# Attention turns written out without a loop, one order of stages, and two GpSimd additions in pieces

## The chip, the cores and the metric

The kernel runs on one core of a Trainium2 chip. The metric is the device time of one launch in microseconds (us). Engines are named as the profile names them: PE is TensorE (PEld its weight loads), DVE is VectorE, ACT is ScalarE, POOL is GpSimd, SP is SyncE, which here only issues DMAs.

## The reference, cut to what matters

One language model block over 32 sequences of 512 tokens, 256 features wide, 16 heads of 16 features:

```
h = emb[x] + (lora_A[:, x].T @ lora_B.T) * 2
n = layernorm(h)
q, k, v = split(n @ Wqkv + bqkv)
local  = softmax(q k / 4, only |i - j| <= 64) @ v
glob   = softmax(q k[first 64] / 4) @ v[first 64]
gate   = sigmoid(n @ Wg + bg)
h = h + ((1 - gate) * local + gate * glob) @ Wout + bout
n = layernorm(h)                       # then the routed part
probs = softmax(n @ router_w.T); top 2 of 8 experts, each with a capacity
h = h + n + sum over the 2 of prob * (silu(n @ w1[e]) @ w2[e])
```

## The kernel before, in words

There are three blocks. A short one prepares weights and tables. The second, which the change is about, does embedding, attention and routing, one sequence after another. The third does the eight experts; it keeps its own loops and is not touched.

**Turns.** The second block is a software pipeline. Turn `i` works on six sequences at once: `cur` (i) has its scores, exponentials and outputs, `nxt` (i+1) its queries, keys and row maxima, `far` (i+2) its embedding, `prev` (i-1) its output projection and second norm, `past` (i-2) its routing, `old` (i-3) the writing of its routing table. `turns` runs turns -2 to 3 and 30 to 34 as code written out, and turns 4 to 29 as one loop (`eng.Fori(4, SEQ - 2)`), so its back jump is taken 25 times on each of the five engines. Inside the loop the waits compare a semaphore with a register, and a `sem_inc` on a `carry` semaphore follows many waits on DVE, POOL and SP. These `sem_inc`s also stand in the turns that are written out.

**Order.** Each turn has 20 jobs. `order` yields for job `n` the stages of `BEFORE[n]`, then `exp n`, then a `max`, then a select, a gather or a scatter, then the stages of `AFTER[n]`. Every engine walks the same list and takes from it the stages in which it has a part. Each engine is a queue that executes in order, and semaphores link them.

- `max m`: PE makes band scores into `psS` banks 2 and 3 (L703 to L725), DVE reduces them to row maxima `negm` (L1007, every fifth L1011). PE may not start the next `max` before DVE has read this one.
- `cut g`: four short dependent DVE instructions (L1022, L1025, L1028, L1031) split the maxima of one quarter of the heads into three bf16 parts. `m_rows g`: PE transposes these (L819), ACT copies, SP sends them out and back into the rows that the scores of `exp` read.
- `exp n`: PE scores with the maximum taken off (L745, every fifth L752), ACT exponentiates (L914, L918), POOL zeroes the corners of the band (`sel`, L550 and L552). `out`: PE multiplies with the values (L773, L778).
- `mix q`: PE transposes outputs, DVE scales them (L1106, L1108, L1111), POOL adds the two halves (L585, 128x256).
- `scale 2`, `scale 1`: DVE normalizes `h1` into `x2` (L1202) and `h` into `xn` (L1210), four instructions each. `values`: PE L805. `qk3`: POOL L592.
- `hold`: POOL adds the output bias to `h` for all four token blocks in one instruction (L597, 128x1024). `residual`: POOL adds `x2` to `h1` in one instruction (L602, 128x1024).

In the tables `cut 1`, `cut 2`, `cut 3` and `cut 0` stand in `BEFORE` of jobs 1, 6, 11 and 16, so on DVE each cut comes ahead of the `max` of that job. The `m_rows` of the same number stands in `AFTER` of that job, so on PE it comes behind the same `max`. Between `max 6` and `max 7` of `nxt`, DVE has `scale 1`, and then the last routing instructions (L1093 to L1095).

Of the kernel before, what the change touches and what calls it, by code (L numbers as in the profile page):

```python
# [89 lines left out]
def build(nc, x, emb, lora_a, lora_b, wqkv, bqkv, wout, bout, wg, bg, rw, w1, w2, y):  # L90
# [20 lines left out]
    with outer:  # L111
# [226 lines left out]
        with ExitStack() as mem:  # L338
# [20 lines left out]
            gates = tmp("gates", [P, 2, QB])  # L359
# [73 lines left out]
            k_top, k_rank, k_mix, egate1_done = sem("k_top"), sem("k_rank"), sem("k_mix"), sem("egate1_done")  # L433
            LOADS = 2 * 16
# [6 lines left out]
            def turns(eng, turn):  # L441


                def whole(i):
                    return dict(old=0 <= i - 3 < SEQ, past=0 <= i - 2 < SEQ, prev=0 <= i - 1 < SEQ, cur=0 <= i < SEQ,
                                nxt=0 <= i + 1 < SEQ, far=0 <= i + 2 < SEQ)
# [9 lines left out]
            BEFORE = {  # L456
                1: (("cur", "cut", 1),),
                2: (("prev", "evac", 3),),
                6: (("cur", "cut", 2),),
                9: (("cur", "evac", 0),),  # L460
                11: (("cur", "cut", 3),),
                12: (("cur", "evac", 1),),
                16: (("nxt", "cut", 0), ("norm", "std", None)),
                17: (("cur", "evac", 2),),
            }
            AFTER = {
                0: (("prev", "out", 10), ("cur", "values", 1)),
                1: (("cur", "m_rows", 1), ("prev", "out", 11), ("cur", "values", 2), ("past", "router", None)),
                2: (("nxt", "xn_t", 0), ("nxt", "xn_t", 1), ("past", "top", 0)),
                3: (("cur", "out", 0), ("nxt", "qk", 0), ("nxt", "qk", 1), ("nxt", "qk2", 0), ("nxt", "qk2", 1), ("cur", "kg", 2), ("past", "top", 1)),  # L470
                4: (("nxt", "qk", 2), ("nxt", "qk", 3), ("nxt", "qk2", 2), ("nxt", "qk2", 3), ("nxt", "qk3", 0), ("nxt", "qk3", 1), ("past", "top", 2), ("past", "weights", None)),
                5: (("cur", "out", 1), ("prev", "mix", 0), ("nxt", "qk3", 2), ("nxt", "qk3", 3), ("past", "top", 3)),
                6: (("cur", "m_rows", 2), ("cur", "out", 2), ("prev", "mix", 1), ("past", "top", 4)),
                7: (("prev", "mix", 2),),
                8: (("prev", "mix", 3), ("cur", "kg", 3)),
                9: (("cur", "out", 3), ("cur", "gates", None), ("nxt", "gate", 0), ("past", "top", 5)),
                10: (("cur", "out", 4), ("past", "ahead", None), ("past", "rank", 0), ("prev", "attn_t", 0), ("nxt", "gate", 1)),
                11: (("cur", "m_rows", 3), ("cur", "out", 5), ("prev", "attn_t", 1), ("past", "rank", 1)),
                12: (("prev", "project", 0), ("prev", "project", 1), ("past", "rank", 2)),
                13: (("cur", "out", 6), ("far", "embed", None), ("prev", "stats2", 0), ("nxt", "kg", 0), ("past", "rank", 3)),  # L480
                14: (("far", "lora", 0), ("far", "lora", 1), ("prev", "stats2", 1)),
                15: (("cur", "out", 7), ("far", "stats1", 0), ("far", "stats1", 1)),
                16: (("nxt", "m_rows", 0), ("cur", "out", 8), ("far", "hold", None), ("prev", "scale", 2)),
                17: (("far", "scale", 1), ("past", "rank", 4)),
                18: (("cur", "out", 9), ("prev", "x2_t", 0), ("prev", "x2_t", 1), ("prev", "residual", None), ("nxt", "kg", 1),
                     ("past", "rank", 5)),
                19: (("nxt", "values", 0), ("far", "zgate", None)),
            }
# [6 lines left out]
            def order(on):

                has = lambda flag: on["prev"] or on["far"] if flag == "norm" else on[flag]
                for n in range(JOBS):
                    for flag, stage, arg in BEFORE.get(n, ()):
                        if has(flag):  # L500
                            yield stage, arg
# [1176 lines left out]
```

## Time and profile before

| what | value |
|---|---|
| median of 3 runs | 4374.85 us (4371.02 to 4392.25) |
| the profiled execution | 4373.87 us, of which the span is 4372.2 us |
| PE busy in the span | 3655.6 us (84%) |
| DVE, POOL, ACT busy | 2346.0, 2267.7, 1905.2 us |
| second block | from about 64 us to about 2700 us |

The chain that ended last in the profile starts at about 2700 us, in the third block, so it says nothing of the second. The second block has to be read turn by turn: from one `m_rows` on PE to the same one a turn later, and from what PE waits for in between. `PEclk` is the granted TensorE clock: 1.00 is 2.4 GHz, 0.50 is 1.2 GHz, and a value between is a mean over time at these two.

### The profile page before, as it was taken

The page shows a single profiled execution, that of the slowest core. Times are in us where ns is not written, and L with a number is a line of the kernel's source. Part 1 is how long each engine was busy: PE and PEld are TensorE (multiplying, and loading weights), DVE is VectorE, ACT ScalarE, POOL GpSimd, SP SyncE. Part 2 cuts the span into 40 slices and gives each one's busy share as a digit, 9 for nine tenths or more (in the row PEclk, how much of TensorE's full clock was granted, in tenths as well). Part 3 has the DMA queues.
Part 4 walks back from the last instruction along what each step waited for, and adds up shares of the span by engine and source line. Part 5 has one row for each costly group of instructions (what it writes and reads, how often), then busy time and mean ns, then how long its engine had stood idle before and what let it go on. Part 6 is the DMA issues. An engine that isn't in the chain of part 4 may idle for free. (4 is left out here: it accounts for less than half of the span.)

```text
span 4372.2 us, 126586 instructions
## 1 busy us (share of the span) xinstructions
PE 3655.6 (84%) x47729; PEld 2906.0 (66%) x47730; DVE 2346.0 (54%) x5585; ACT 1905.2 (44%) x3061; POOL 2267.7 (52%) x2467
## 2 busy tenths in 40 slices
PE   2788787777787777777778886699999999999998
PEld 1455455555455455455455554699999999999998
DVE  4576666666666666666666664334343443334333
ACT  1445444444444444444444453344443444334343
POOL 2455565565565565565565555444444444444444
PEclk8898888988888888888888897899999999999999
DMA  5443433433433433433433431323232332322222
GB/s 123 120 126 118 128 101 109 129 102 109 128 103 109 129 103 110 129 102 110 129 102 110 129 102 44 97 45 68 47 67 44 67 67 45 66 46 46 44 45 41
DMA packets 240779, 397.82 MB, mean 91 GB/s; under 512 B 34692, under 2 KB 148820, under 8 KB 240244
## 3 DMA queue, kind: packets, MB, share of 16 engines
q1 hardware_dynamic: 167908, 299.07, 22.3%
q0 software_dynamic: 70512, 91.16, 11.9%
q8 instruction: 359, 5.88, 0.7%
q10 hardware_dynamic: 1952, 1.31, 0.1%
q14 instruction: 48, 0.39, 0.0%
HBM read 198.55 MB, written 192.88 MB: 90 GB/s over the span
## 5 line engine op out<-in xcount | busy, mean ns | idle before, releaser
L1390 POOL DMA_INDIRECT out_y<-out_t,tok_out x264 | 425.3, 1611 | 773.9 <-DMA out_y<-out_t,tok_out 386.9
L1536 ACT ACTIVATE act<-psS 128x512 f32<-128x512 f32 x528 | 316.6, 600 | 916.4 <-PE psS L1464 898.4
L1598 DVE TENSOR_TENSOR h_lo<-act,h_hi 128x512 fp32r<-128x512 f32 x528 | 367.9, 697 | 584.8 <-ACT h_hi L1537 578.6
L550 POOL TENSOR_SCALAR_AFFINE_SELECT pl<-pl 128x512 f32<-128x512 f32 x512 | 330.5, 646 | 676.6 <-ACT pl L914 674.7
L914 ACT ACTIVATE pl<-psS 128x896 f32<-128x896 f32 x512 | 469.2, 916 | 480.2 <-PE psS L745 472.9
L1499 PE MATMUL psO<-w_hi,h_hi 128*128 128x256 f32 x2112 | 598.6, 283 | 0.9 <-DVE h_lo L1598 0.9
L1499 PE MATMUL psO<-w_lo,h_hi 128*128 128x256 f32 x2112 | 588.7, 279 | 0.0
L1499 PE MATMUL psO<-w_hi,h_lo 128*128 128x256 f32 x2112 | 587.6, 278 | 0.0
L1007 DVE TENSOR_REDUCE negm<-psS 128x4 f32<-128x640 f32 x512 | 419.3, 819 | 295.8 <-PE psS L719 246.1
L1464 PE MATMUL psS<-xg_hi,w_hi 128*128 128x256 f32 x1984 | 551.7, 278 | 0.2 <-issue 0.2
L1464 PE MATMUL psS<-xg_hi,w_lo 128*128 128x256 f32 x1984 | 551.3, 278 | 0.0
L1464 PE MATMUL psS<-xg_lo,w_hi 128*128 128x256 f32 x1984 | 551.2, 278 | 0.0
L1499 PEld LDWEIGHTS psO<-w_hi,h_hi 128*128 128x128 f32 x2112 | 397.1, 188 | 1.1 <-DVE h_lo L1598 1.1
L1499 PEld LDWEIGHTS psO<-w_lo,h_hi 128*128 128x128 f32 x2112 | 397.0, 188 | 0.0
L1499 PEld LDWEIGHTS psO<-w_hi,h_lo 128*128 128x128 f32 x2112 | 395.5, 187 | 0.0
L745 PE MATMUL psS<-Q,K 102*32 102x160 bf16 (+2 forms) x8192 | 271.2, 252 | 127.9 <-issue 79.8
L1464 PEld LDWEIGHTS psS<-xg_hi,w_hi 128*128 128x128 f32 x1984 | 374.9, 189 | 0.4 <-issue 0.4
L1464 PEld LDWEIGHTS psS<-xg_lo,w_hi 128*128 128x128 f32 x1984 | 372.5, 188 | 0.0
L1464 PEld LDWEIGHTS psS<-xg_hi,w_lo 128*128 128x128 f32 x1984 | 372.4, 188 | 0.0
L745 PEld LDWEIGHTS psS<-Q,K 102*32 102x32 bf16 x8192 | 166.5, 105 | 303.4 <-issue 198.6
L703 PE MATMUL psS<-K,Q 96*32 96x160 bf16 (+2 forms) x8192 | 278.7, 243 | 88.7 <-DVE negm L1007 63.0
L552 POOL TENSOR_SCALAR_AFFINE_SELECT pl<-pl 128x512 f32<-128x512 f32 x512 | 329.7, 644 | 0.0
(229 smaller groups left out, 8021.2 us busy)
## 6 DMA issues: line engine op xcount, KB each, us to landing
qk_scr<-qk SPq DMA_DIRECT2D x64, 768.0 KB
Q<-qk_scr SPq DMA_DIRECT2D x128, 384.0 KB, 4.6
K<-qk_scr SPq DMA_DIRECT2D x128, 384.0 KB, 5.4
qk_scr<-qk SPq DMA_DIRECT2D x64, 512.0 KB
h_rows<-held SPq DMA_DIRECT2D x32, 512.0 KB
qk_scr<-qk SPq DMA_DIRECT2D x64, 256.0 KB
hb<-h_rows SPq DMA_DIRECT2D x32, 512.0 KB
x_rows<-x SPq DMA_DIRECT2D x32, 512.0 KB
```

The costliest lines, as they stand in the source:

```text
L550: pool.affine_select(out=cols[:, :, 0:P], in_=cols[:, :, 0:P], compare_op=ALU.is_ge, fill=0.0, base=0, pattern=[[0, 4], [1, P]], channel_m ...
L552: pool.affine_select(out=cols[:, :, P:WIN], in_=cols[:, :, P:WIN], compare_op=ALU.is_ge, fill=0.0, base=0, pattern=[[0, 4], [-1, P]], chan ...
L703: pe.matmul(psS[SUB * c:SUB * (c + 1), 2 + a, q % 2 * BAND + lo:q % 2 * BAND + hi], Q[0:ROWS, 4 * g + 2 * v + a, (4 * q + c) * SUB:(4 * q ...
L745: last = pe.matmul(psS[SUB * c:SUB * (c + 1), a, j % 2 * WIN + SUB * c + lo:j % 2 * WIN + SUB * c + hi], K[0:ALL, 4 * g + 2 * v + a, key:k ...
L914: act.activation(pl[:, v, half, :, lo:hi], psS[:, 0:2, lo:hi], ACT.Exp, scale=SCALE).then_inc(exp_done, 1)
L1007: dve.tensor_reduce(negm[:, g, 0, v, :, 2 * half:2 * half + 2], psS[:, 2:4, 0:2 * BAND].rearrange("p a (q u) -> p a q u", u=BAND), AX.X, A ...
L1390: pool.indirect_dma_start(out=y[:, :], in_=out_t[:, tile.out, s, :], in_offset=None, out_offset=bass.IndirectOffsetOnAxis(ap=tok_out[:, ti ...
L1464: last = pe.matmul(psS[:, f // 2, (f % 2) * 256:(f % 2) * 256 + cols], w[:, tile.par, k, fs], x[:, k, 0:cols], start=(k == 0 and n == 0), ...
L1499: last = pe.matmul(psO[:, s, 0:D], h_[:, f, ts], w[:, tile.par, f, :], start=(f == 0 and n == 0), stop=(f == FT - 1 and n == 2))
L1536: act.activation(act32[:, b, :, 0:cols], src, ACT.Silu)
L1598: dve.tensor_tensor(h_lo[:, 2 * b:2 * b + 2, 0:cols], act32[:, b, :, 0:cols], h_hi[:, 2 * b:2 * b + 2, 0:cols].bitcast(F32), ALU.subtract) ...
```

## The change

1. `turns`, `Fori`, the `BEFORE` and `AFTER` tables and the `carry` semaphores go. Each engine has a written list of stages for one turn (`ORDER`), and Python writes out all turns from -3 to 35. All waits compare with constants. Which `psX` bank a stage uses is counted along PE's list instead of read from a table.
2. On PE, ACT, POOL and SP the lists keep the order of before. On DVE each of the four cuts moves behind the next `max`. Nothing else changes places.
3. `hold` and `residual` become four instructions of 128x256 each; the first pieces of `hold` wait for the first half of `h` alone. The DMAs of their results still wait for all four.
4. `gates` has two buffers. `top 5` is written as four stages with the same instructions.

PE at the end of a loop turn: the last `max` of `nxt`, `values 0`, then the jump. Before:

```order
L713 MATMUL psS<-mask,identb 32x32 x2
L719 MATMUL psS<-mask,identb 32x2x2x32 x8
L805 MATMUL psX<-wv_sb,xn_t 128x256 x4
L450 REGISTER_ALU
L450 COMPARE_AND_BRANCH
```

Now, with `exp 0` of the next turn right behind (L681 and L687 are the masks, L767 the values, L713 the scores of `exp`):

```order
L681 MATMUL psS<-mask,identb 32x32 x2
L687 MATMUL psS<-mask,identb 32x2x2x32 x8
L767 MATMUL psX<-wv_sb,xn_t 128x256 x4
L713 MATMUL psS<-Q,K 32x96
L713 MATMUL psS<-Q,K 32x128
```

The jump and the register step ahead of it are gone.

DVE at the start of a loop turn, `max 9`, `cut 1`, `max 10`, before (`ISA` and `REGISTER_ALU` rows are waits, `sem_inc`s and register steps):

```order
L1011 TENSOR_REDUCE negm<-psS 128x16
L87 ISA
L1022 CAST m_cut<-negm 128x32
L1023 ISA
L1025 TENSOR_TENSOR m_rest<-negm,m_cut 128x32
L1026 REGISTER_ALU
L1028 CAST m_cut<-m_rest 128x32
L1029 REGISTER_ALU
L1031 TENSOR_TENSOR m_cut<-m_rest,m_cut 128x32
L1002 REGISTER_ALU
L87 ISA
L1007 TENSOR_REDUCE negm<-psS 128x2x2
```

Now (L956 is `max 9`, L952 `max 10`, L967 to L975 the cut, L1072 the copy of the router's result):

```order
L956 TENSOR_REDUCE negm<-psS 128x16
L952 TENSOR_REDUCE negm<-psS 128x2x2
L967 CAST m_cut<-negm 128x32
L971 TENSOR_TENSOR m_rest<-negm,m_cut 128x32
L973 CAST m_cut<-m_rest 128x32
L975 TENSOR_TENSOR m_cut<-m_rest,m_cut 128x32
L1072 COPY logit<-psX 128x32
```

The cut stands behind `max 10`, and the same holds for `cut 2` and `max 15`, `cut 3` and `max 0` of `nxt`, `cut 0` and `max 5` of `nxt`.

The diff, cut to its core:

```diff
-            def turns(eng, turn):
-                for i in range(-2, 4):
-                    turn(i, whole(i))
-                with eng.Fori(4, SEQ - 2) as i:
-                    turn(i, whole(4))
-                for i in range(SEQ - 2, SEQ + 3):
-                    turn(i, whole(i))
...
+            ORDER["dve"] = (
+                ("cur", "max", 9), ("cur", "max", 10), ("cur", "cut", (1, 0)), ("cur", "cut", (1, 1)), ("cur", "cut", (1, 2)),
...
+            def order(name):
+                for i in range(-3, SEQ + 4):
+                    for flag, stage, arg in ORDER[name]:
+                        if 0 <= i + REL[flag] < SEQ:
+                            yield stage, arg, i + REL[flag]
+
+            BANK, used = {}, 0
+            for stage, arg, s in order("pe"):
+                if stage not in ("exp", "max", "out"):
+                    BANK[stage, arg, s] = used % 2
+                    used += stage != "mix"
...
-                            if stage == "hold":
-                                pool.wait_ge(h_done, 2 * (far + 1))
-                                need(pool, hold_out, 16 * far)
-                                pool.tensor_tensor(held[:, :, :], h[:, :, :], bout_b[:, :].unsqueeze(1).to_broadcast([P, QB, D]),
-                                                   ALU.add).then_inc(held_done, 1)
-                            if stage == "residual":
-                                pool.wait_ge(x2_done, QB * (prev + 1))
-                                pool.tensor_tensor(h1[:, :, :], h1[:, :, :], x2[:, :, :], ALU.add).then_inc(res_done, 1)
...
+                        if stage == "hold":
+                            pool.wait_ge(h_done, 2 * s + arg // 2 + 1)
+                            if arg == 0:
+                                need(pool, hold_out, 16 * s)
+                            pool.tensor_tensor(held[:, arg, :], h[:, arg, :], bout_b[:, :], ALU.add).then_inc(held_done, 1)
+                        if stage == "residual":
+                            pool.wait_ge(x2_done, QB * s + arg + 1)
+                            pool.tensor_tensor(h1[:, arg, :], h1[:, arg, :], x2[:, arg, :], ALU.add).then_inc(res_done, 1)
...
                         whole = negm[:, g, :, :, :, :].rearrange("p k v a q -> p (k v a) q")
-                        dve.wait_ge(max_done, JOBS * s + 5 * (g + 1))
-                        need(dve, m_t_ready, done)
-                        dve.sem_inc(carry["dve"], 1)
-                        dve.tensor_copy(m_cut[:, 0, :, :], whole).then_inc(k_cut, 1)
-                        dve.wait_ge(k_cut, 3 * done + 1)
-                        dve.sem_inc(carry["dve"], 1)
-                        dve.tensor_tensor(m_rest[:, :, :], whole, m_cut[:, 0, :, :], ALU.subtract).then_inc(k_cut, 1)
-                        dve.wait_ge(k_cut, 3 * done + 2)
...
+                        if part == 0:
+                            dve.wait_ge(max_done, JOBS * s + 5 * (g + 1))
+                            need(dve, m_t_ready, done)
+                            dve.tensor_copy(m_cut[:, 0, :, :], whole).then_inc(k_cut, 1)
+                            return
+                        dve.wait_ge(k_cut, 3 * done + part)
+                        if part == 1:
+                            dve.tensor_tensor(m_rest[:, :, :], whole, m_cut[:, 0, :, :], ALU.subtract).then_inc(k_cut, 1)
+                        if part == 2:
+                            dve.tensor_copy(m_cut[:, 1, :, :], m_rest[:, :, :]).then_inc(k_cut, 1)
+                        if part == 3:
+                            dve.tensor_tensor(m_cut[:, 2, :, :], m_rest[:, :, :], m_cut[:, 1, :, :], ALU.subtract).then_inc(cut_done, 1)
```

## Rows read from the trace of the kernel before

**Rows 1.** The page: PE busy in tenths in 40 slices of the span.
```profile
PE   2788787777787777777778886699999999999998
```

**Rows 2.** Stretches: start:end, length, busy (count) PE, PEld, DVE, ACT, POOL; PEclk, DMA, GB/s.
```profile
276.90:430.60 153.70, 126.18 (x2167) 82.13 (x2156) 106.62 (x266) 76.79 (x115) 87.16 (x110) 0.90 0.39 121
430.60:2482.20 2051.60, 1632.62 (x26913) 1051.05 (x26904) 1306.89 (x3325) 952.76 (x1426) 1190.89 (x1475) 0.88 0.38 114
2482.20:2559.60 77.40, 62.68 (x1089) 40.11 (x1080) 52.12 (x133) 38.09 (x59) 45.44 (x56) 0.91 0.40 118
276.90:299.60 22.70, 19.05 (x302) 11.33 (x290) 14.32 (x34) 13.61 (x23) 12.78 (x16) 1.00 0.49 172
1004.90:1029.60 24.70, 20.96 (x306) 12.81 (x294) 13.46 (x34) 13.81 (x23) 12.95 (x16) 0.93 0.46 158
1066.50:1089.40 22.90, 17.20 (x254) 11.65 (x257) 13.91 (x32) 8.41 (x13) 9.61 (x12) 0.70 0.38 113
334.20:352.40 18.20, 14.88 (x257) 10.34 (x258) 13.79 (x32) 7.85 (x13) 9.49 (x12) 0.83 0.44 135
```

**Rows 3.** Waits of PE from 431 to 2482 us: total, times, longest.
```profile
PE psX L819 <- DVE m_cut L1031: 170.2, 69, 3.5
PE psS L745 <- issue: 78.2, 30, 4.5
PE psS L703 <- DVE negm L1007: 47.4, 28, 2.7
```

**Rows 4.** Timeline, PE at two turn ends (start, us, what): written out, loop.
```profile
344.04 0.72 PE L703 MATMUL psS<-K,Q 96*32 96x160 bf16 x16 [2.73 <-DVE negm L1007]
344.90 3.13 PE L805 MATMUL psX<-wv_sb,xn_t 128*128 128x256 f32 x8
347.96 0.46 PE L745 MATMUL psS<-Q,K 102*32 102x96 bf16 x16
...
1082.62 0.72 PE L745 MATMUL psS<-Q,K 102*32 102x96 bf16 x16 [4.19 <-issue]
```

**Rows 5.** Timeline, PE and DVE around `m_rows 1`.
```profile
352.37 0.22 PE L719 MATMUL psS<-mask,identb 128*32 128x128 bf16 x2
352.53 0.22 PE L819 MATMUL psX<-identb,m_cut 128*24 128x128 bf16 x1
...
352.63 0.82 DVE L1007 TENSOR_REDUCE negm<-psS 128x4 f32<-128x640 f32 x1 [0.73 <-PE psS L719]
```

**Rows 6.** Timeline, DVE and POOL at `cut 2`.
```profile
1028.55 0.97 DVE L1031 TENSOR_TENSOR m_cut<-m_rest,m_cut 128x32 bf16<-128x32 f32 x1
1027.21 2.26 POOL L592 TENSOR_TENSOR qk<-qk_rest,qk 128x512 bf16<-128x512 f32 x2
```

**Rows 7.** Timeline, DVE and PE at `cut 3`.
```profile
1047.00 0.20 DVE L1025 TENSOR_TENSOR m_rest<-negm,m_cut 128x32 f32<-128x32 f32 x1 [0.15 <-DVE m_cut L1022]
1047.93 0.29 PE L819 MATMUL psX<-identb,m_cut 128*24 128x128 bf16 x2 [1.32 <-DVE m_cut L1031]
```

**Rows 8.** Timeline, DVE and POOL at `cut 0`.
```profile
1065.03 0.35 DVE L1022 CAST m_cut<-negm 128x32 bf16<-128x32 f32 x1
1062.98 2.35 POOL L597 TENSOR_TENSOR held<-h,bout_b 128x1024 f32<-128x1024 f32 x1
```

**Rows 9.** DVE and POOL between `max 6` and `max 7`; L1210 and L585 over the run (min/median/max ns).
```profile
1070.26 4.22 DVE L1210 TENSOR_SCALAR xn<-h,mv,rstd 128x256 f32<-128x256 f32 x4
1071.31 2.39 POOL L602 TENSOR_TENSOR h<-h,x 128x1024 f32<-128x1024 f32 x1
L1210 DVE TENSOR_SCALAR xn<-h,mv,rstd x128: 399/718/2454, 86.2 to 2549.5; 128x256 f32<-128x256 f32 x128
L585 POOL TENSOR_TENSOR attn<-mix x128: 713/729/742, 223.5 to 2703.1; 128x256 f32<-128x256 f32 x128
```

**Rows 10.** Timeline, one DVE instruction under three of POOL.
```profile
1041.56 1.57 DVE L1145 TENSOR_SCALAR gates<-gate_new 128x4 f32<-128x4 f32 x1
```

More of the change, by code:

```diff
@@ L358, in build @@
             gate_new = tmp("gate_new", [P, QB])
[L359 removed]
+            gates = tmp("gates", [P, 2, 2, QB])
             qk1 = tmp("qk1", [P, 4, T], BF16)
@@ L456, in build @@
[L456 to L488, printed above, removed]
@@ L495, in order @@
[L495 to L501, printed above, removed]
-                    if on["cur"]:
-                        yield "exp", n
-                    if n < NEXT_MAX:
-                        if on["cur"]:
-                            yield "max", (0, n + JOBS - NEXT_MAX)
-                    elif on["nxt"]:
-                        yield "max", (1, n - NEXT_MAX)
-                    if on["cur"] and n and (n - 1) % 5 < 4:
-                        yield "sel", n - 1
-                    if on["far"] and n < 2 * QB:
-                        yield "gather", n
-                    if on["old"] and 2 * QB <= n < 4 * QB:
-                        yield "scatter", n - 2 * QB
-                    for flag, stage, arg in AFTER[n]:
-                        if has(flag):
-                            yield stage, arg
+            REL = {"old": -3, "past": -2, "prev": -1, "cur": 0, "nxt": 1, "far": 2, "next": 3}
@@ L521, in edges @@
                 return (64 if block == 0 else 0), (WIN - 64 if block == QB - 1 else WIN)
-            class Bank:
-                def __init__(self):
-                    self.last = [None, None]
-                def take(self, pe, b, i, signal, per, k, rel):
-                    if self.last[b] is not None:
-                        s, p_, k_, r_ = self.last[b]
-                        pe.wait_ge(s, p_ * (i + r_) + k_)
-                    self.last[b] = (signal, per, k, rel)
-                def next_turn(self):
-                    self.last = [x and (*x[:3], x[3] - 1) for x in self.last]
@@ L682, in _ @@
-                    turns(sp, turn)
+                        if stage == "load":
+                            g = arg
+                            sp.wait_ge(qk_out, QK_OUT * (s + 1))
+                            if s > 0:
+                                sp.wait_ge(st_ready, JOBS * (s - 1) + 5 * (g + 1))
+                            for part, into in enumerate((Q, K)):
+                                sp.dma_start(into[0:ROWS, 4 * g:4 * (g + 1), :], qk_scr[part, :, 4 * g:4 * (g + 1), :]).then_inc(quarter_in[g], 16)
@@ L687, in _, with take @@
                 def _(pe):
-                    bank = Bank()
+                    freed = [None, None]
+                    def take(key, signal, count, banks=None):
+                        for b in (BANK[key],) if banks is None else banks:
+                            if freed[b] is not None:
+                                pe.wait_ge(*freed[b])
+                            freed[b] = (signal, count)
                     def max_tile(s, m):
```

908 lines of the change are left out of this document (454 added, 454 removed).

## The prediction, made before the changed kernel ran

> **What bounds the kernel now.** I began with the slices of the page [rows 1]: PE is busy seven or eight tenths in the first 25 slices (the second block, the one that changes) and nine tenths behind them. The chain that ended last lies wholly in the third block, so for the second block I took stretches instead. The first loop turn's `m_rows 1` stands at 430.6 us and the last one's at 2482.2 us, 25 jumps apart, and PE is busy 1632.62 of these 2051.60 us, 80% [rows 2]. A pass of the loop so takes 82.06 us. The list of what PE waits for in that stretch [rows 3] has two large entries and a third: 170.2 us for the last instruction of a cut on DVE (6.8 us a pass), 78.2 us before L745 where nothing is found that it waited for ("issue", 3.1 us a pass), and 47.4 us in L703 for DVE's maxima (1.9 us a pass). So the block is a ping-pong in which PE is the longest engine and stops for DVE at known places; what delays a cut delays PE, and what shortens DVE between two maxima helps PE.
>
> **The loop goes.** Turns that are written out stand in the same trace. From `m_rows 1` at 276.9 to the one two turns later it takes 153.70 us, 76.85 a turn, and behind the loop one turn takes 77.40 [rows 2]; together 231.1 / 3 = 77.0. The loop pass is 5.0 us longer. The place is seen: from `values 0` to `exp 0` PE has no gap where the turn is written out (347.96), and 4.19 us of "issue" at the jump (1082.62) [rows 4]. The stretch from `m_rows 0` to `m_rows 1` that holds this point takes 22.90 us in the loop against 18.20 written out, at a granted clock of 0.70 against 0.83 [rows 2]: 4.7 us, 4.2 of it the gap, the rest the slower clock behind it. The register steps and `sem_inc`s within a turn cost PE nothing that I can find: `m_rows 1` to `m_rows 2` is 24.70 us in the loop and 22.70 written out, but at 0.93 and 1.00 of the clock [rows 2]. The written-out samples lack a little (the scatters in one half turn, a gather in the last), so I take 4.9 us, between 4.7 and 5.0. 25 x 4.9 = 122 us gone. What is late next at that place is `max 8` of `nxt`, which already waits 2.73 us for DVE when written out [rows 4].
>
> The Trainium skill (Runtime: NRT & Kernel Launch, section Instruction fetch mechanics) says that a taken branch breaks the sequential prefetch of instructions and can stall for a fetch, while straight code is streamed and a crossing from one block of instructions to the next is mostly hidden. The gap at the jump agrees; the second half of the rule speaks against rival 4 below.
>
> **The cuts move behind a max.** On PE `m_rows g` stands right behind the same `max` that the cut now follows on DVE. So PE has to wait for that max's reduction (0.82 us) and then the whole cut. The four instructions of a cut take at the least 0.18 to 0.20 us each (the second one 0.20 [rows 7]), 0.76 us in all, and the 0.15 us of gap between them [rows 7] should shrink, since the `sem_inc` there goes; I take 0.05, so 0.9 us a cut, and bounds of 0.76 and 1.2.
> - `m_rows 1`: today the cut is over before PE gets there and PE has no idle time [rows 5]. Now: the last mask matmul ends at 352.59, the reduction runs 352.63 to 353.45 [rows 5], the cut to about 354.3, and PE goes on at 354.3 to 354.4. That is 1.7 us; a select of POOL runs there too and can stretch two of the four by about 0.3 each, up to 2.4. I take 2.1. PE has no other gap until the stall at `m_rows 2`, so nothing takes this up.
> - `m_rows 2`: the last instruction of cut 2 already takes 0.97 us since POOL's two `qk3` additions run from 1027.21 to 1029.47 [rows 6]. 0.82 us later one instruction of the four falls out of their shadow. I take 0.45, between 0.25 and 0.8.
> - `m_rows 3`: PE stops 1.32 us until 1047.93 [rows 7], so its `max` ended at 1046.61. The reduction then ends at about 1047.5, the cut at 1048.3, and PE goes on at 1048.4, or later under the select of POOL that begins there: 0.4 to 0.9, I take 0.65.
> - `m_rows 0`: the cut starts at 1065.03 and the long addition `held` ends at 1065.33 [rows 8]. The reduction comes first now, most of the rest of `held` passes under it: 0 to 0.6, I take 0.2.
>
> Together 3.4 us a turn (2.35 to 4.7). Behind each stalled `m_rows` stand the outputs, `exp` and `max` of the next job, so ACT, POOL and DVE all shift with PE; the later DMA of the rows of a quarter shifts too. After the cut DVE no longer owes a max, but at all four places it waits for PE anyway: nothing comes back.
>
> **The additions in pieces.** Between `max 6` and `max 7` DVE normalizes `xn` in 4.22 us, and the residual addition takes 2.39 us from 1071.31 [rows 9]. One of the four is held for as long, up to 2.454 us, where 0.40 is the least [rows 9]. A piece of 128x256 should cost what L585 costs, 0.73 us [rows 9], so four take 2.9 us instead of 2.39. The third `xn` then ends near 1072.1 instead of 1073.8, 1.7 us earlier; the two routing instructions behind it now meet the later pieces, which gives back some 0.6. I take 1.1 us gained a turn, and PE waits long enough for this max to feel all of it [rows 3, 4]. The bounds: 1.6 gained if only one piece is in the way, and 0.5 lost if DVE cannot get in between pieces. For the second speaks one row: L1145, four elements a partition, takes 1.57 us under three POOL instructions that follow each other without a gap [rows 10]. For the first speaks that the last part of cut 2 gets in as soon as one of the two `qk3` additions ends [rows 6]. `hold` in pieces is in `m_rows 0` above. POOL's 0.55 us more per addition lies in its idle time: it is busy 1190.89 of 2051.60 us [rows 2].
>
> The Trainium skill (SBUF — State Buffer, section Who interferes with whom) says that VectorE and GpSimd share one pair of ports, that whoever is first holds it for the whole instruction and that the other is blocked that long. By that rule each DVE instruction waits for one piece at most and the gain is 1.1 to 1.6; the row of L1145 goes beyond the rule, and by it the term is a loss of 0.5. The rest of the sum does not change.
>
> **The clock.** Two stretches with the same instructions take 22.70 us at 1.00 and 24.70 at 0.93 [rows 2]: a time at 1.2 GHz costs nearly 2 us there, since PE has no slack. The clock has fallen behind stalls of the size that `m_rows 1` now gets (it stands at 0.83 on average in the stretch that holds the 2.73 us stall [rows 2, 4]). I take that it comes in four turns of ten: 0.8 us a turn, bounds 0 and 1.8.
>
> **The sum.** Per turn 3.4 - 1.1 + 0.8 = 3.1 us more, in 31 turns (32 sequences, the first and last turns being partly filled): 96 us. 122 - 96 = 26 us less. The profiled execution took 4373.87 us (1 us under the median of the runs), so 4348 us. `gates`, the split of `top 5`, and the bank count move no instruction and cost nothing: the banks come out alternating as before.
>
> **Rivals.** The gain of the loop is firm, the price per turn is not: at 122 / 31 = 3.9 us a turn it eats all.
> 1. Cheap cuts: 2.7 us for the four, 1.6 gained by the pieces, no clock term: 1.1 a turn, 34 us. 4374 - 122 + 34 = 4286. For it speaks that each has a lower bound near this; against it that all must hit at once.
> 2. No net change: the cuts as forecast, but the pieces bring nothing: 3.4 + 0.8 = 4.2 a turn, 130 us, 4382.
> 3. Slower, by the clock: the stall at `m_rows 1` brings a time at 1.2 GHz into the stretch behind it in every turn, and the longer stalls at `m_rows 2` and `3` one more: 3.4 - 1.1 + 3.4 = 5.7 a turn, 177 us, 4429. It decides once the clock costs over 1.6 us a turn. For it: the loop turns run at 0.88 and the clock drops at stalls. Against it: that it has room to drop only where a stall and little work meet.
> 4. The change does not do what it says: straight code must be fetched too, and what goes at the jump comes back as waits of PE's sequencer elsewhere. Then 4374 + 96 = 4470. Against it: no such wait in the written-out turns [rows 2, 4].
>
> **Numbers.** Forecast 0.50 (own range 4323 to 4373), rival 1 0.17, rival 2 0.15, rival 3 0.12, rival 4 0.06. 0.5% of this time is 22 us, about what a measurement can tell from no change: 4353 and 4397 are the borders. Half of the forecast's case and a little more lies below 4353. Faster: 0.30 + 0.17 = 0.47. Same: 0.20 + 0.12 = 0.32. Slower: 0.03 + 0.12 + 0.06 = 0.21. The range 4283 to 4405 holds the forecast's case, most of rivals 1 and 2 and a little of 3: 0.80.
>
> **What would show it.** From one `m_rows 1` of PE to the next: 80 us in a full turn (82.06 in the loop now, 77.0 written out). No "issue" gap before the first L745 scores of a turn. A wait of PE for the cut at `m_rows 1` of about 2 us, where there is none, and at `m_rows 3` of about 2 instead of 1.3. The longest `xn` instruction near 0.75 us instead of 2.45, and PE's wait for `max 7` down from 2.7 to about 1.6. The mean clock of the second block stays near 0.88. The prediction is wrong if a full turn takes under 78.5 or over 81.5 us, or if PE's wait at `m_rows 1` is under 1.5 us.

## The result, and the profile after

The changed kernel takes 4486.84 us (median of 4 runs, 4484.45 to 4494.93), the kernel before 4375.89 us beside it: 1.025 times as long, 95% interval 1.022 to 1.028. Forecast were 4348 us, 26 less than before. For e12 further down, two of its ten runs (4620.95 and 13444.82 us) were disturbed, and its time and interval are those of the other eight. The profiled execution has a span of 4482.6 us, 110 us more than before.

The slices of the page look as before ([rows 1]): sevens and eights in the second block, nines behind it.

```profile
PE   2777877877787777787887887599999999999999
```

The stretches (columns as in [rows 2]): the first is most of the second block, then one turn from `m_rows 0` to the next, and its four stretches `m_rows 0` to 1, 1 to 2, 2 to 3, 3 to 0.

```profile
400.00:2500.00 2100.00, 1667.33 (x26608) 1071.40 (x26600) 1306.50 (x3288) 947.88 (x1404) 1193.81 (x1608) 0.85 0.36 109
1036.30:1121.70 85.40, 67.64 (x1077) 43.07 (x1078) 52.73 (x134) 38.40 (x58) 48.31 (x65) 0.84 0.36 109
1036.30:1055.30 19.00, 14.53 (x256) 9.93 (x256) 12.99 (x32) 9.18 (x14) 11.67 (x18) 0.86 0.46 136
1055.30:1080.20 24.90, 20.62 (x288) 11.92 (x288) 14.38 (x33) 12.84 (x21) 11.79 (x15) 0.91 0.44 152
1080.20:1100.30 20.10, 14.33 (x268) 9.21 (x268) 13.92 (x34) 6.92 (x10) 14.71 (x21) 0.84 0.38 103
1100.30:1121.70 21.40, 18.16 (x265) 12.01 (x266) 11.44 (x37) 9.46 (x13) 10.15 (x14) 0.74 0.16 41
```

A turn takes 85.4 us, where the loop pass took 82.06 and the written-out turns of before 77.0 [rows 2]. The clock of the block is 0.85 where it was 0.88. The stretch that held the jump is 19.0 us instead of 22.90, so the loop did give its time back; every other stretch is longer, and the last one runs at 0.74.

What PE waits for from 547 to 2484 us, which are nearly 23 turns (total, times, longest; answers to [rows 3]):

```profile
PE psX L779 <- DVE m_cut L975: 263.1, 91, 4.3
PE psX L789 <- DVE mix L1061: 25.3, 33, 0.9
PE psS L671 <- DVE negm L952: 23.9, 19, 2.0
PE psS L693 <- DVE negm L952: 21.4, 23, 1.1
```

The "issue" entry before the scores of `exp 0` (L745, now L713) is gone. The wait for the cut was 170.2 us in 69 waits in 25 turns, 6.8 us a turn; now it is 263.1 us in 91 waits in nearly 23 turns, 11.6 us a turn: four waits a turn instead of three.

PE at the turn's end (answers to [rows 4]): the wait for `max 7`, its values, and `exp 0` with no gap where 4.19 us stood.

```profile
1045.79 0.45 PE L671 MATMUL psS<-K,Q 96*32 96x160 bf16 x16 [1.70 <-DVE negm L952]
1046.29 1.99 PE L767 MATMUL psX<-wv_sb,xn_t 128*128 128x256 f32 x8
1048.21 0.46 PE L713 MATMUL psS<-Q,K 102*32 102x96 bf16 x16
```

PE and DVE around `m_rows 1` (answers to [rows 5]):

```profile
1052.51 0.34 PE L687 MATMUL psS<-mask,identb 128*32 128x128 bf16 x8
1055.33 0.50 PE L779 MATMUL psX<-identb,m_cut 128*24 128x128 bf16 x3 [2.49 <-DVE m_cut L975]
1055.53 1.07 PE L746 MATMUL psO<-pg,V 128*32 128x512 f32 x3
1055.74 1.91 PE L746 MATMUL psO<-pg,V 128*32 128x512 f32 x5
...
1052.89 0.82 DVE L952 TENSOR_REDUCE negm<-psS 128x4 f32<-128x640 f32 x1 [2.13 <-PE psS L687]
1053.63 0.61 DVE L967 CAST m_cut<-negm 128x32 bf16<-128x32 f32 x1
1054.28 0.56 DVE L971 TENSOR_TENSOR m_rest<-negm,m_cut 128x32 f32<-128x32 f32 x1
1054.87 0.18 DVE L973 CAST m_cut<-m_rest 128x32 bf16<-128x32 f32 x1
1055.09 0.19 DVE L975 TENSOR_TENSOR m_cut<-m_rest,m_cut 128x32 bf16<-128x32 f32 x1
```

The wait is there as foreseen: reduction, four short instructions, two of them stretched, 2.49 us in all. New are the outputs behind it: three L746 take 1.07 us, five 1.91. Keep these two rows for the experiments.

DVE, PE and POOL at `cut 3` and `m_rows 3` (answers to [rows 7]):

```profile
1098.57 1.47 DVE L973 CAST m_cut<-m_rest 128x32 bf16<-128x32 f32 x1
1100.32 0.50 PE L779 MATMUL psX<-identb,m_cut 128*24 128x128 bf16 x3 [2.99 <-DVE m_cut L975]
1098.77 0.64 POOL L542 TENSOR_SCALAR_AFFINE_SELECT pl<-pl 128x512 f32<-128x512 f32 x1
1099.36 0.64 POOL L544 TENSOR_SCALAR_AFFINE_SELECT pl<-pl 128x512 f32<-128x512 f32 x1
```

The third instruction of the cut, least 0.18 us, is held 1.47 us under two selects of POOL that follow each other (L542, L544), and PE waits 2.99 us instead of 1.32. In 20 of the 24 turns summed below it is held 1.45 us or more.

`xn` between `max 6` and `max 7`, the residual in pieces, and the two lines over the whole run (answers to [rows 9]):

```profile
1126.27 2.87 DVE L1156 TENSOR_SCALAR xn<-h,mv,rstd 128x256 f32<-128x256 f32 x4
1126.75 2.97 POOL L592 TENSOR_TENSOR h<-h,x 128x256 f32<-128x256 f32 x4
L1156 DVE TENSOR_SCALAR xn<-h,mv,rstd x128: 395/811/880, 83.9 to 2657.3; 128x256 f32<-128x256 f32 x128
L592 POOL TENSOR_TENSOR h<-h,x x128: 719/769/816, 276.3 to 2840.3; 128x256 f32<-128x256 f32 x128
```

The four `xn` take 2.87 us instead of 4.22, none is held longer than 0.88 us where one was held 2.45, and PE's wait for this max is 1.70 us where it was 2.73 in a written-out turn. That part did what it should. DVE does get in between pieces here. The Trainium skill says of the ports that VectorE and GpSimd share (SBUF — State Buffer, section Who interferes with whom) that whoever issues first has them for its whole instruction while the other is blocked. Read as one instruction of POOL at most, as the prediction read it, this fits `xn`, but not the 1.47 us under two selects of 0.64.

### The profile page after: what moved, and what is told of

It reads as the page before. It is cut to its first block and busy times, and to the rows that moved or that the text cites. A ratio compares the mean times of both kernels' runs of the same rounds, so it can differ in the third digit from the quotient of the medians.

```text
span 4482.6 us, 119129 instructions
## 1 busy us (share of the span) xinstructions
PE 3729.4 (83%) x47729; PEld 2947.1 (66%) x47730; DVE 2360.6 (53%) x5585; ACT 1914.8 (43%) x3061; POOL 2289.1 (51%) x2659
## 5 line engine op out<-in xcount | busy, mean ns | idle before, releaser
L542 POOL TENSOR_SCALAR_AFFINE_SELECT pl<-pl 128x512 f32<-128x512 f32 x512 | 331.2, 647 | 753.8 <-ACT pl L865 753.0
L952 DVE TENSOR_REDUCE negm<-psS 128x4 f32<-128x640 f32 x512 | 418.8, 818 | 465.3 <-PE psS L687 404.3
L779 PE MATMUL psX<-identb,m_cut 128*24 128x128 bf16 x512 | 68.0, 275 | 366.2 <-DVE m_cut L975 366.2
L671 PE MATMUL psS<-K,Q 96*32 96x160 bf16 (+2 forms) x8192 | 297.9, 256 | 62.0 <-DVE negm L952 38.0
L544 POOL TENSOR_SCALAR_AFFINE_SELECT pl<-pl 128x512 f32<-128x512 f32 x512 | 325.5, 636 | 0.0
L713 PE MATMUL psS<-Q,K 102*32 102x160 bf16 (+2 forms) x8192 | 278.6, 257 | 51.6 <-ACT pl L865 32.3
```

Of the source, the lines that this page charges most:

```text
L542: pool.affine_select(out=cols[:, :, 0:P], in_=cols[:, :, 0:P], compare_op=ALU.is_ge, fill=0.0, base=0, pattern=[[0, 4], [1, P]], channel_m ...
L544: pool.affine_select(out=cols[:, :, P:WIN], in_=cols[:, :, P:WIN], compare_op=ALU.is_ge, fill=0.0, base=0, pattern=[[0, 4], [-1, P]], chan ...
L671: pe.matmul(psS[SUB * c:SUB * (c + 1), 2 + a, q % 2 * BAND + lo:q % 2 * BAND + hi], Q[0:ROWS, 4 * g + 2 * v + a, (4 * q + c) * SUB:(4 * q ...
L713: last = pe.matmul(psS[SUB * c:SUB * (c + 1), a, j % 2 * WIN + SUB * c + lo:j % 2 * WIN + SUB * c + hi], K[0:ALL, 4 * g + 2 * v + a, key:k ...
L779: last = pe.matmul(psX[0:24, b, q * P:(q + 1) * P], m_cut[:, :, :, q].rearrange("p l x -> p (l x)"), identb[:, :], start=True, stop=True, ...
L952: dve.tensor_reduce(negm[:, g, 0, v, :, 2 * half:2 * half + 2], psS[:, 2:4, 0:2 * BAND].rearrange("p a (q u) -> p a q u", u=BAND), AX.X, A ...
```

## The experiments

Two causes compete for the 8.2 us a turn between 77.0 and 85.2: the waits themselves, and the clock. To weigh them I took 24 turns of each trace (the 6th to the 29th) and summed, per turn: its length; PE's waits before the four `m_rows` (order 1, 2, 3, 0); and the time at 1.2 GHz, from the same clock records from which the windows' mean is made. For a check: a mean of 0.85 means 2 x (1 - 0.85) = 30% at 1.2 GHz, 25.6 of 85.2 us.

| kernel | turn us | waits at `m_rows` 1, 2, 3, 0 | us at 1.2 GHz | run, us | ratio to before (interval) |
|---|---|---|---|---|---|
| before | 82.05 | 0, 3.54, 1.11, 2.26 | 20.5 | 4375.89 | |
| changed | 85.24 | 2.49, 4.01, 3.00, 2.05 | 26.0 | 4486.84 | 1.025 (1.022 to 1.028) |
| e1 cuts ahead | 74.36 | 0, 3.39, 1.27, 2.59 | 10.2 | 4150.63 | 0.9503 (0.9487 to 0.9519) |
| e2 loop, cuts behind | 89.32 | 2.66, 4.70, 2.78, 3.19 | 23.6 | 4599.61 | 1.0527 (1.0510 to 1.0545) |
| e3 whole additions | 79.23 | 2.49, 4.01, 2.13, 1.86 | 11.5 | 4338.53 | 0.9934 (0.9908 to 0.9961) |
| e4 idle matmuls | 75.06 | 0.66, 0.54, 0.03, 1.33 | 1.4 | 4190.73 | 0.9591 (0.9575 to 0.9607) |
| e5 ahead, whole | 76.31 | 0, 3.42, 0.85, 1.85 | 12.9 | 4210.44 | 0.9622 (0.9594 to 0.9651) |
| e6 ahead, idle matmuls | 73.40 | 0, 0, 0.03, 0.32 | 3.8 | 4131.95 | 0.9448 (0.9422 to 0.9475) |
| e7 idle at `m_rows 1` | 82.36 | 0.66, 4.11, 3.04, 2.12 | 17.5 | 4405.94 | 1.0064 (1.0037 to 1.0090) |
| e8 idle matmuls, whole | 78.84 | 0.66, 0.53, 0.70, 0.56 | 4.4 | 4299.33 | 0.9833 (0.9804 to 0.9862) |
| e9 fewer idle matmuls | 73.99 | 0, 0, 0.03, 1.26 | 4.8 | 4144.33 | 0.9478 (0.9454 to 0.9502) |
| e10 cut 1 ahead | 79.07 | 0, 4.02, 2.95, 2.02 | 17.6 | 4304.25 | 0.9837 (0.9812 to 0.9862) |
| e11 held whole | 85.18 | 2.49, 4.00, 2.96, 2.03 | 24.9 | 4494.35 | 1.028 (1.025 to 1.031) |
| e12 cut 3 ahead | 82.09 | 2.49, 4.02, 0.85, 1.98 | 23.2 | 4376.26 | 1.0009 (0.9993 to 1.0024) |

The kernel before, run beside each group of four, had medians of 4369.33, 4372.87 and 4369.95 us. The turns and waits are those of one profiled execution each; the runs of e3 lie 55 us apart.

### e1: the cuts back ahead of their max

```diff
+            def cuts_ahead(items):
+                items = list(items)
+                for g, m in ((1, ("cur", "max", 10)), (2, ("cur", "max", 15)), (3, ("nxt", "max", 0)), (0, ("nxt", "max", 5)),):
+                    block = [x for x in items if x[1] == "cut" and x[2][0] == g]
+                    items = [x for x in items if x not in block]
+                    at = items.index(m)
+                    items[at:at] = block
+                return tuple(items)
+            ORDER["dve"] = cuts_ahead(ORDER["dve"])
```

> The changed kernel with one edit: on DVE the four cuts stand ahead of their max again, as before the change; no loop, additions in pieces. Theory T (the new place of the cuts costs 4.6 us a turn of waits of PE and about 4.5 us a turn of slower TensorE clock, and the loop's jump was worth about 5 us a turn): a full turn of 76 to 77 us, 4225 us, range 4200 to 4270. Rival U (code written out is itself slower in the steady state, and the cuts cost only the waits): 4487 - 31 x 4.6 = 4344 us. If T holds this beats both kernels.

4150.63 us, 336 less than the changed kernel, and 49 us under the range of theory T (4200 to 4270): 10.9 us a turn, where the waits at the four `m_rows` differ by 4.3. PE at `m_rows 1`: no wait, and the outputs behind it (here L756) at twice the speed, 0.63 and 1.02 us for three and five.

```profile
1006.81 0.27 PE L789 MATMUL psX<-identb,m_cut 128*24 128x128 bf16 x2
1006.87 0.63 PE L756 MATMUL psO<-pg,V 128*32 128x512 f32 x3
1006.92 0.22 PE L789 MATMUL psX<-identb,m_cut 128*24 128x128 bf16 x1
1006.98 1.02 PE L756 MATMUL psO<-pg,V 128*32 128x512 f32 x5
```

So the order of the cuts is the loss, and more than half of it is not in the waits.

### e2: the loop of before, with the cuts behind

```diff
-                        if has(flag):
+                        if has(flag) and stage != "cut":
                             yield stage, arg
...
                         yield "max", (1, n - NEXT_MAX)
+                    for flag, stage, arg in BEFORE.get(n, ()):
+                        if has(flag) and stage == "cut":
+                            yield stage, arg
```

> The kernel before, loop and long additions kept, with one edit: on DVE each cut stands behind the max. T: waits of 4.6 us a turn more, 143 us, 4518 us at the least; the loop's turns already run 20 us each at 1.2 GHz, so the clock adds less than in written-out code, 4518 to 4600, I say 4560. U: 4518 us, no slower clock than before.

4599.61 us, 230 more than before: the move of the cuts costs time in the loop too, and needs nothing else of the change. (Written out it costs 336 us beside the pieces, e1 to the changed kernel, and 128 us beside whole additions, e5 to e3.) Of 7.3 us a turn the waits are 6.4, and the time at 1.2 GHz is 3.1 us more. Theory T said 4560 and 4518 to 4600: the measured time stands at the very end of its range. U's 4518 is out.

### e4, e7: the same waits, filled with idle matmuls

If the clock is the rest, PE busy with anything during the waits should bring it back. In front of its wait for the cut, PE computes a product that nobody reads into the bank that the stage owns and then overwrites: 8, 14, 10 and 6 of 128x512 at `m_rows` 1, 2, 3 and 0. e7 does so at `m_rows 1` alone, 8 of them.

```diff
-                            pe.wait_ge(cut_done, QUARTERS * s + arg + 1)
                             take(key, m_t_done, QUARTERS * s + arg + 1)
+                            for _ in range({1: 8, 2: 14, 3: 10, 0: 6}[arg]):
+                                pe.matmul(psX[:, b, :], identb[:, :], mask[:, :, :, :].rearrange("p a b u -> p (a b u)")[:, 0:512],
+                                          start=True, stop=True, skip_group_check=True)
+                            pe.wait_ge(cut_done, QUARTERS * s + arg + 1)
```

> The changed kernel with idle matmuls (identity times a constant tile, 128x512 bf16, results overwritten) ahead of PE's wait at each m_rows: 8, 14, 10 and 6 of them at m_rows 1, 2, 3 and 0, each 0.2 to 0.4 us, about as long as PE waits there. They take nothing off any wait. T: the clock stays at 2.4 GHz more, so the kernel gets faster although it does more: 60 to 120 us, 4370 to 4430 us, with under 15 us a turn at 1.2 GHz in place of 27. U: no gain, 4487 to 4520 us.

> The changed kernel with the 8 idle matmuls at m_rows 1 alone. If a stall slows the stretch right behind it (theory C, local), m_rows 1 to m_rows 2 goes from 26.0 to about 23.5 us and the rest stays: 4487 - 31 x 2.5 = 4410 us. If the drops of the clock hang together over a turn (one moves the next), the other stretches get shorter too: 4250 to 4350 us. If the stall at m_rows 1 is not the cause: 4487 us.

e4: 4190.73 us, 296 less than the changed kernel with the same order of work on DVE, and with more work on PE. The theory had the sign, but expected only 60 to 120 us. PE at `m_rows 1`, and the same turn's stretches (whole turn, then `m_rows` 1 to 2, 2 to 3):

```profile
956.78 1.90 PE L778 MATMUL psX<-mask,identb 128*128 128x512 bf16 x8
959.33 0.35 PE L782 MATMUL psX<-identb,m_cut 128*24 128x128 bf16 x3 [0.66 <-DVE m_cut L978]
959.47 0.63 PE L746 MATMUL psO<-pg,V 128*32 128x512 f32 x3
959.57 1.02 PE L746 MATMUL psO<-pg,V 128*32 128x512 f32 x5
```

```profile
941.90:1017.30 75.40, 66.84 (x1115) 41.53 (x1116) 53.85 (x134) 38.10 (x58) 48.27 (x65) 0.98 0.41 124
959.30:982.70 23.40, 22.31 (x302) 12.68 (x302) 14.40 (x33) 12.84 (x21) 11.83 (x15) 1.00 0.45 161
982.70:999.60 16.90, 13.77 (x279) 8.62 (x280) 13.11 (x34) 6.93 (x10) 13.63 (x19) 1.00 0.45 123
```

The eight take 1.90 us of the wait, PE still waits 0.66 us for the same DVE instruction, so the cut comes no sooner; the clock behind it is 1.00 and the outputs take 0.63 and 1.02. 24.6 us less at 1.2 GHz and 10.2 us less a turn: 0.41 us for each. e7 tells that this is local: the stretch from `m_rows` 1 to 2 falls from 26.0 to 23.5 us, at a clock of 1.00,

```profile
1022.90:1046.40 23.50, 19.11 (x288) 11.41 (x289) 14.38 (x33) 12.83 (x21) 11.90 (x15) 1.00 0.47 160
```

and the kernel by 81 us, 2.6 a turn, as expected (4410, measured 4405.94).

### e10, e12: one cut ahead

The function of e1 with `(1, ("cur", "max", 10))` alone, and with `(3, ("nxt", "max", 0))` alone.

> The changed kernel with cut 1 alone put ahead of its max; cuts 2, 3 and 0 stay behind theirs. Local theory (each late cut costs its own wait and the slow clock in the stretch behind it): the wait of 2.5 us at m_rows 1 goes, and of the 6.3 us at 1.2 GHz between m_rows 1 and 2 all but 0.2, at 0.41 us each 2.5 us; together 5.0 x 31 = 155 us: 4332 (4310 to 4360). Rival (the clock falls elsewhere instead, as it depends on the whole turn): only the wait goes, 4487 - 77 = 4410.

> The changed kernel with cut 3 alone put ahead of its max; cuts 1, 2 and 0 stay behind theirs. Local theory: the wait at m_rows 3 falls from 3.0 us to about 1.3, and the slow clock between m_rows 3 and 0 (8.9 us, 0.9 with all cuts ahead) by 4 to 8 us at 0.41 us each: 1.7 + 1.6 to 3.3 = 3.3 to 5.0 us a turn, 102 to 155 us: 4330 to 4385, say 4358. Rival (the clock falls elsewhere instead): only the wait goes, 4487 - 53 = 4434.

e10: 4304.25 us, 183 less than the changed kernel: more than the local theory's 155, 6 us under its range (4310 to 4360), and far from the rival's 77. Its stretch from `m_rows` 1 to 2 stands at 1.00:

```profile
990.30:1013.70 23.40, 19.13 (x308) 11.41 (x296) 15.21 (x34) 13.62 (x23) 13.40 (x17) 1.00 0.49 167
```

Of the 5.9 us a turn 2.5 are the wait, the rest is the clock (8.4 us less at 1.2 GHz, 3.4 us at 0.41 each). e12: 4376.26 us, 111 less, 3.6 a turn, inside the local forecast (4330 to 4385); 2.15 of them are the wait, and 2.8 us less at 1.2 GHz are 1.1. Cut 1 so costs more than cut 3, and the difference is mainly in the clock (3.4 and 1.1 us a turn), not in the wait (2.5 and 2.15). The two together are 293 of the 336 us.

### e3, e11: the additions whole again

e3 takes both additions back to one instruction, e11 only `held`.

```diff
-                            pool.wait_ge(h_done, 2 * s + arg // 2 + 1)
-                            if arg == 0:
-                                need(pool, hold_out, 16 * s)
-                            pool.tensor_tensor(held[:, arg, :], h[:, arg, :], bout_b[:, :], ALU.add).then_inc(held_done, 1)
+                            pool.wait_ge(h_done, 2 * (s + 1))
+                            need(pool, hold_out, 16 * s)
+                            pool.tensor_tensor(held[:, :, :], h[:, :, :], bout_b[:, :].unsqueeze(1).to_broadcast([P, QB, D]),
+                                               ALU.add).then_inc(held_done, 1)
...
-                            pool.tensor_tensor(h1[:, arg, :], h1[:, arg, :], x2[:, arg, :], ALU.add).then_inc(res_done, 1)
+                            pool.tensor_tensor(h1[:, :, :], h1[:, :, :], x2[:, :, :], ALU.add).then_inc(res_done, 1)
```

> The changed kernel with the two GpSimd additions whole again (128x1024), all else kept. T: max 6 to max 7 on DVE takes 4.94 us now and 5.75 before, so the pieces save 0.8 us a turn and this is 25 us slower, 4510 us, range 4480 to 4540. Rival V (the pieces do harm through POOL's longer hold of the ports): faster than 4487 by over 10 us.

> The changed kernel with the addition held = h + bout whole again (one of 128x1024) and the residual still in four pieces. The held addition ends just before m_rows 0, the residual runs after it. If the 148 us between the changed kernel and the one with both whole hang on what stands before m_rows 0 (its stretch has 8.9 us at 1.2 GHz against 3.4): near 4340. If they hang on the residual, whose pieces let max 6 and 7 run sooner: near 4487. If both count: between, about 4410.

e3 missed by far: 4338.53 us (4320.31 to 4375.28), 148 less than the changed kernel, not more, as the rival V had it. e11 gives 4494.35 us, as the changed kernel: all of it is the residual. DVE is worse off in e3, as it must be: `xn` takes 4.05 us again, and PE waits 2.65 us for `max 7` and then 2.49 at `m_rows 1`, as in the changed kernel.

```profile
996.90 4.05 DVE L1156 TENSOR_SCALAR xn<-h,mv,rstd 128x256 f32<-128x256 f32 x4
998.42 2.39 POOL L592 TENSOR_TENSOR h<-h,x 128x1024 f32<-128x1024 f32 x1
1002.85 0.72 PE L671 MATMUL psS<-K,Q 96*32 96x160 bf16 x16 [2.65 <-DVE negm L952]
1013.96 0.35 PE L779 MATMUL psX<-identb,m_cut 128*24 128x128 bf16 x3 [2.49 <-DVE m_cut L975]
1014.09 0.63 PE L746 MATMUL psO<-pg,V 128*32 128x512 f32 x3
```

But the outputs behind this wait take 0.63 us, not 1.07. PE's two largest waits in the same 24 turns of e3 (536 to 2439 us), then one whole turn and its stretches 1 to 2, 2 to 3, 3 to 0:

```profile
PE psX L779 <- DVE m_cut L975: 251.6, 96, 4.0
PE psS L671 <- DVE negm L952: 63.1, 24, 2.7
```

```profile
994.00:1072.50 78.50, 60.92 (x1077) 39.65 (x1078) 54.15 (x133) 38.18 (x58) 47.62 (x59) 0.93 0.39 119
1014.00:1037.30 23.30, 19.07 (x288) 11.34 (x288) 14.38 (x33) 12.84 (x21) 11.73 (x15) 0.99 0.47 162
1037.30:1055.40 18.10, 12.91 (x268) 8.24 (x268) 12.90 (x33) 6.93 (x10) 13.43 (x19) 0.92 0.42 115
1055.40:1072.50 17.10, 15.22 (x265) 10.49 (x266) 12.43 (x37) 9.70 (x14) 11.07 (x13) 0.90 0.21 52
```

The same wait of 2.49 us, ended by the same instruction, has 0.99 behind it here and 0.91 in the changed kernel (over the 24 turns, 1.2 and 6.3 us at 1.2 GHz between `m_rows` 1 and 2). 14.5 us less of a turn is at 1.2 GHz, worth 5.9 us at 0.41, and the turn is 6.0 us shorter. All waits of PE in a turn, not only those at the `m_rows`, come to 17.6 us in both kernels, so what is left for the 6.0 us is the clock. The pieces did not cost work; with them the clock fell more often.

One thing of the waits did change. At `cut 3`, L973 takes 0.18 us in all 24 turns of e3, where it takes 1.45 us or more in 20 of the 24 turns of the changed kernel, and the wait at `m_rows 3` is 2.13 instead of 3.00 us. Whether a cut meets the selects of POOL depends so on what else the turn holds.

### e5, e8: what the pieces are worth when the clock is not in the way

e5 is e1 with whole additions, e8 is e4 with whole additions.

> Code written out, cuts ahead of their max, and the two GpSimd additions whole again: of the change only the loop's end is left. Theory C (the pieces save 0.8 us a turn of DVE time themselves; that they cost 148 us beside the late cuts came through the TensorE clock alone): 4151 + 25 = 4176 us, range 4150 to 4205, with 10 to 14 us a turn at 1.2 GHz. Rival P (the pieces cost time themselves, on POOL or at the ports): faster than 4151 by 50 us or more.

> e4_warm with the additions whole: cuts late, the clock held up by idle matmuls. Both are near 2.4 GHz all the time, so the difference to e4_warm (4191) is what the pieces do without the clock. C: 0.8 us a turn saved by the pieces, so this is 25 us slower, 4215 us, range 4200 to 4235. P: faster than 4191.

e5 is 60 us slower than e1 (1.9 us a turn), e8 is 109 us slower than e4 (3.5 a turn). Both go the way opposite to e3, so the theory that the pieces cost time by themselves falls. The clock theory has the sign right and the sizes too small: e5 stands 5 us beyond its range, e8 84 us above its number and 64 beyond its range. e8's turn has 3.0 us more at 1.2 GHz than e4's, 1.2 us at 0.41, so about 2.3 us of its 3.5 is the later work itself.

The four written-out kernels without idle matmuls, side by side:

| | cuts ahead | cuts behind |
|---|---|---|
| whole additions | e5: 4210.44 us, 12.9 us a turn at 1.2 GHz | e3: 4338.53 us, 11.5 |
| pieces | e1: 4150.63 us, 10.2 | changed: 4486.84 us, 26.0 |

Each edit taken alone went the way that the prediction said, and the cuts by its size: the cuts behind cost 128 us (forecast with its clock term 3.4 + 0.8 = 4.2 a turn, 130 us), the pieces save 60 (forecast 34), and the loop's end saves 162 (forecast 122). By their sum the changed kernel would be 94 us faster than before. It is slower because the two edits together cost 208 us more than one and one, and 17.2 us more of a turn at 1.2 GHz; at 0.41 that is 7.1 us a turn, 219 us in 31 turns.

### e6, e9: the best of both

e6 is e1 with 14, 4 and 8 idle matmuls at `m_rows` 2, 3 and 0; e9 has 4 in place of 8.

> Code written out, cuts ahead, additions in pieces, and idle matmuls (results overwritten) ahead of PE's waits at m_rows 2, 3 and 0: 14, 4 and 8 of them, none at m_rows 1 where PE does not wait. C: 10.2 us a turn at 1.2 GHz fall to about 2; at 0.41 us lost for each (10.2 us a turn gained for 24.6 us in e4_warm) that is 3.3 us a turn, 100 us: 4045 us, range 4020 to 4090. Rival: with the cuts ahead the slow time lies where PE waits anyway, no gain: 4140 to 4160.

> The written-out program with the cuts ahead and idle matmuls, 4 in place of 8 at m_rows 0, 14 at m_rows 2 and 4 at m_rows 3 as in e6. Theory A (e6's eight matmuls overran the wait at m_rows 0, where e1 waits 2.6 us: its stretch from m_rows 3 to m_rows 0 takes 18.1 us against 17.1 in e1, while the next one gains 1.1): 0.5 to 1 us a turn back, 4132 - 31 x 0.75 = about 4109 (4095 to 4125). Rival B (the stretch from m_rows 3 to 0 is bound by the other engines and would stay at 18): 4125 to 4140, no change from e6.

e6: 4131.95 us, 0.9448 of before, the fastest of all; e9 4144.33. The intervals of the two overlap, and e6's and e1's lie just apart (0.9475, 0.9487). For e6 the first theory expected 4045 and failed; the rival (no gain) expected 4140 to 4160. 6.4 us less at 1.2 GHz brought 1.0 us a turn (0.15 each, not 0.41). From `m_rows` 1 to 2 the turn takes 22.8 us in both e1 and e6, and in e6 PE has only 0.35 us left of its waits at the four `m_rows`. From `m_rows` 3 to 0 it takes 18.05 us, 17.1 in e1. e9 asked whether the eight idle matmuls at `m_rows 0` had overrun the wait there, and expected 4109 us if so, and 4125 to 4140 if other engines bind the stretch. They had not: with four of them PE waits 1.26 us for the cut again, but the stretch still takes 18.0 us. What holds it there, and with it the small gain of e6, is open. PE's largest wait in e6 is that for a max:

```profile
PE psS L681 <- DVE negm L965: 43.2, 24, 1.8
PE psS L723 <- ACT pl L878: 39.0, 48, 1.4
```

## Why the prediction was wrong

It said 26 us faster; it is 111 us slower. The step that failed is the clock term, 0.8 us a turn where 4.6 came, set as if the prices of the two edits could be added. By its steps:

- **The loop.** 4.9 us a turn gone: right in kind (no gap at L713), and somewhat small in size. Before against e5, which has the old order on all engines and whole additions, and new only the written-out turns (without the `sem_inc`s, and with the second buffer of `gates`), is 4372.87 to 4210.44 us, 162 instead of 122. With the cuts behind, the same step is worth 261 us (e2 to e3).
- **The cuts, direct.** `m_rows 1` was priced at 2.1 us, bounds 1.7 to 2.4, and measured 2.49; `m_rows 2` at 0.45, measured 0.47; `m_rows 0` at 0.2, measured -0.2. `m_rows 3` was priced at 0.65 and measured 1.9 (3.00 against 1.11). The working saw the select that begins there, but not that the cut could be held through two in a row (1.47 us), though the row of L1145 showed a case of it [rows 10] and I used that for the pieces alone; in e3, where that hold is absent, it measured 1.0 (2.13 against 1.11). Sum 4.65 instead of 3.4, inside the bounds of 2.35 to 4.7.
- **The pieces.** 1.1 us gained a turn: right where it was looked for. PE's wait for `max 7` fell by 1.0 us against the written-out turn (over 24 turns, from 2.63 us in e3 to 1.12), the longest `xn` to 0.88. The value of the pieces in the whole kernel is another thing: 60 us gained with the cuts ahead, 148 us lost with the cuts behind.
- **The clock.** This is the step that failed. The term was 0.8 us a turn, bounds 0 to 1.8, on the ground that the clock falls in four turns of ten. Time at 1.2 GHz is 26.0 us a turn now, and was 14.9 in the written-out turns of before (means of 0.90 and 0.91 in 153.70 and 77.40 us [rows 2]: 2 x 0.10 x 153.70 + 2 x 0.09 x 77.40 = 44.7 us in three turns). 11.1 us more at 0.41 is 4.6 us a turn, 141 us in 31 turns, where 25 had been set.

The corrected sum is 77.0 + 4.65 + 4.6 - 1.0 = 85.25 us a turn; measured 85.24. That the two agree so closely is luck: the 1.0 is one pair of rows, and the 0.41 is an estimate from e4. Nor is the 4.6 the price of the late cuts as such: beside whole additions they brought no more time at 1.2 GHz (12.9 us a turn in e5, 11.5 in e3). Rival 3 had the mechanism and the right sign. It fell 58 us short, since it too set the clock at 3.4 us and `m_rows 3` at 0.65. I gave it 0.12 although its condition, over 1.6 us a turn, lay inside the bounds of my own term. What was said against it, that the clock drops only where a stall and little work meet, rested on one pair of stretches, and I asked only for the stall at `m_rows 1`. In the trace of after the worst stretch is not behind that one but from `m_rows` 3 to 0, at 0.74. And in the list of what would show it the clock "stays near 0.88": 0.85 is the sign that it did not.

Rival 4 (straight code must be fetched) is refuted: e1 is the same straight code and has 4150 us. The Trainium skill (Runtime: NRT & Kernel Launch, section Instruction fetch mechanics) says that straight code is streamed and that its crossings are mostly hidden; e1 agrees.

Shown is that the time at 1.2 GHz takes the larger part of what the late cuts cost in the changed kernel (e4: same order, waits filled, 296 us back), that in this kernel it is attached to single waits (e7, e10), and that it accounts for the loss with the residual in pieces (e3, e11). Open is what makes the same 2.49 us wait pull the clock down in the changed kernel and not in e3. The difference that I can see is the longer wait for `max 7` some 10 us ahead of it (2.65 against 1.70 us), behind which the clock is already down in e3 (its 16 L671 take 0.72 us, those of the changed kernel 0.45). That the clock was just down is not enough to spare the stretch. The clock came back between 5.5 and 8.5 us ahead of `m_rows 1` in all 24 turns of e3, and it fell again at this wait in 2 of them; it came back in the same place in 17 of 24 turns of e12, and fell again in all 17. At this same wait of 2.49 us it fell in 22 of 24 turns of the changed kernel, 20 of e11 and 24 of e12 (during the wait or within 2 us of its end). So the wait alone does not decide either, and whether the moment at which it comes does, no run here separates. I also did not take cuts 2 and 0 apart (43 us are left for the two and for how all four act together).

## What to carry to other kernels

Where PE is the longest engine and waits in short stops, price each new wait twice: once as itself, and once as the slower clock of the stretch behind it. Here that was 3.4 us a turn for the 2.5 us wait of cut 1 and 1.1 for the 2.15 of cut 3, but nothing for the same late cuts beside whole additions, so give it a wide range. Before a piece of work is put between two engines' hand-overs, ask which engine waits for its end: a cut that four other instructions need goes ahead of a max that nobody is waiting for yet. And do not add the prices of two edits that both change PE's waits: the pieces saved 60 us alone and cost 148 beside the late cuts.

## What was not expected of the hardware

- Useless matmuls in a wait made the kernel 6.6% faster (4486.84 to 4190.73 us). 26.0 us of a turn were at 1.2 GHz without them and 1.4 with them. The Trainium skill (TensorE: Matmul & The Clock Gate, Part 1) says that the clock gate follows how busy PE has been; this trace agrees. Its example is of waits for a DMA that come with every tile; here the waits are of 2 to 4 us for DVE, in a block where PE was busy 1667.33 of 2100.00 us.
- The price of a time at 1.2 GHz was not fixed. By the turns it was 0.41 us for each in e4 and 0.15 in e6; both are estimates.
- A DVE instruction of 0.18 us was held 1.47 us, through two selects of POOL of 0.64 us each, while no `xn` beside the four pieces took over 0.88 us, its least 0.40 included. In e3 the same instruction met no select and took 0.18.
- The same wait of PE, 2.49 us for the same instruction, had the clock fall at it in 22 of 24 turns of one kernel and in 2 of 24 of another (e3).
